# One quarter of each attention pair's products on GpSimd, and a chunk's steps behind the pair's transposes on TensorE

## The reference, cut to what matters

```python
att = softmax(einsum('bhxd,bhyd->bhxy', q, k) * SCALE)
att = softmax(att * mask)            # mask is 0.5 where row % 64 == column % 64, else 1
out = einsum('bhxy,bhyd->bhxd', att, v)
t   = t + (out @ w_out.T + b_out)    # per image, over all 12 heads
```

## Time and profile before

| | |
|---|---|
| runs | 462.84, 463.34, 464.28 us; median 463.34 |
| the profiled execution | 467.23 us, of which 465.4 us are the span from the first to the last instruction |
| busy in the span | PE 425.2 us (91%), DVE 225.7 (48%), ACT 158.6 (34%), POOL 125.3 (27%) |
| first and last second exponential (L691) | 192.21 and 273.38 us: the attention loop is 81 us of the span |
| granted TensorE clock, mean | 0.989 of 2.4 GHz |

### The profile page before, as it was taken

How to read it: one execution, slowest core, us unless ns; L and a number is a source line. 1 busy time by engine, 2 the same in 40 slices (tenths; PEclk the granted TensorE clock), 3 DMA queues, 4 the chain that set the end, 5 groups by cost and what they waited for, 6 DMA issues and landing times.

```text
span 465.4 us, 7581 instructions
## 1 busy us (share of the span) xinstructions
PE 425.2 (91%) x2303; PEld 303.3 (65%) x2304; DVE 225.7 (48%) x611; ACT 158.6 (34%) x399; POOL 125.3 (27%) x136
## 2 busy tenths in 40 slices
PE   0999989999999899988888779998999999999995
PEld 0755356666667888766676547555777777777784
DVE  3536342222222576889889764462533333333333
ACT  1033141222221145988778733211221212221210
POOL 3201044545554000000000000011354444554430
PEclk9999999999999999999999998799999999999999
DMA  8999001111100792000000697600110011100006
GB/s 229 274 311 295 20 24 45 37 38 40 42 23 1 210 355 107 1 0 2 2 1 0 161 241 191 190 10 3 32 34 27 23 29 37 38 28 14 0 0 203
DMA packets 18056, 38.62 MB, mean 83 GB/s; under 512 B 4420, under 2 KB 13892, under 8 KB 17586
## 3 DMA queue, kind: packets, MB, share of 16 engines
q1 hardware_dynamic: 9570, 29.66, 22.6%
q0 software_dynamic: 5280, 6.32, 4.8%
q10 hardware_dynamic: 3184, 2.36, 1.6%
HBM read 35.16 MB, written 7.67 MB: 92 GB/s over the span
## 4 chain that ended last, share of the span: by engine, by line
PE 83%; ACT 6%; DMA 5%; DVE 3%; issue 2%; ACTq 0%; DVEq 0%; SPq 0%; POOLq 0%
PE bank L1250 17%; PE bank L1265 14%; PE bank L1183 12%; PE bank L1244 8%; PE bank L1434 5%; PE bank L1257 4%; PE bank L1388 4%; DMA w_first<-y_rows 3%; PE bank L1450 3%; PE bank L1226 2%; PE bank L1169 2%; PE bank L1482 2%; ACT scratch L691 2%; ACT g_sh L691 2%; ACT xn_t L691 2%
## 5 line engine op out<-in xcount | busy, mean ns | idle before, releaser
L1250 PE MATMUL bank<-w_first,rows_t 96*128 x248 | 85.3, 487 | 0.2 <-issue 0.2
L521 POOL DMA_INDIRECT rows<-xn_rows,slot_tok x56 | 57.3, 1024 | 94.1 <-DVE slot_tok L871 32.5
L529 POOL DMA_INDIRECT y_rows<-y,slot_row x54 | 55.3, 1024 | 98.9 <-DVE y L939 58.3
L1265 PE MATMUL bank<-w_second,hid_t 128*128 x370 | 70.1, 329 | 4.6 <-DVE hid_t L924 2.8
L1265 PEld LDWEIGHTS bank<-w_second,hid_t 128*128 128x128 f32 x370 | 58.7, 190 | 7.1 <-issue 7.0
L1250 PEld LDWEIGHTS bank<-w_first,rows_t 96*128 96x128 f32 x248 | 44.7, 190 | 25.2 <-issue 0.4
L929 DVE TENSOR_TENSOR act_h<-bank,act_g 128x384 f32<-128x384 f32 x31 | 17.3, 558 | 59.1 <-PE bank L1250 59.1
L1244 PE MATMUL bank<-w_first,rows_t 96*128 (+1 forms) x92 | 43.5, 594 | 1.1 <-issue 1.0
L625 ACT ACTIVATE act_g<-bank 128x384 f32<-128x384 f32 x31 | 15.2, 491 | 72.2 <-PE bank L1250 72.2
L941 DVE TENSOR_TENSOR y<-bank,w_second 128x192 f32<-128x192 f32 x23 | 8.2, 358 | 63.7 <-PE bank L1265 63.7
L567 POOL COPY act_h<-o_inv 128x256 f32<-128x256 f32 x12 | 4.8, 402 | 122.3 <-DVE o_inv L1070 122.3
(11 more groups left out here) (181 smaller groups left out, 645.8 us busy)
## 6 DMA issues: line engine op xcount, KB each, us to landing
w_first<-in_gate_up SPq DMA_DIRECT2D x16, 576.0 KB, 9.4
w_second<-in_down SPq DMA_DIRECT2D x1, 4608.0 KB, 19.0
w_first<-in_fc SPq DMA_DIRECT2D x1, 3072.0 KB
w_second<-in_fc SPq DMA_DIRECT2D x1, 3072.0 KB, 28.5
rows<-xn_rows,slot_tok POOLq DMA_INDIRECT x56, 2.6
y_rows<-y,slot_row POOLq DMA_INDIRECT x54, 2.3
w_first<-in_x_t SPq DMA_DIRECT2D x2, 384.0 KB, 4.8
w_first<-in_w SPq DMA_DIRECT2D x1, 768.0 KB, 7.0
```

The source lines that it names most:

```text
L521: pool.indirect_dma_start(rows[b % 2][:], None, xn_rows[L.l], bass.IndirectOffsetOnAxis(slot_tok[:, b:b + 1].bitcast(U32), 0), bounds_chec ...
L529: pool.indirect_dma_start(y_rows[L.l], bass.IndirectOffsetOnAxis(slot_row[:, b:b + 1].bitcast(U32), 0), y[b % 2][:], None, bounds_check=TO ...
L1250: ins = pe.matmul(bank[:, 5 + g, 0:I1], rows_t[0:CH, k, :], w(CH, (k * 2 + g) * I1, I1), start=(k == 0), stop=(k == NCH - 1))
L1265: ins = pe.matmul(bank[:, 1, 0:C], hid_t[:, tile(ic)], w(P, ic * C, C), start=(ic == 0), stop=(ic == L.IC - 1))
```

## The change

- `attention(p)` on DVE does three of the four products. The fourth quarter goes to POOL, as two instructions in place: `fourth(p)` multiplies by the mask (`tensor_tensor`), waits for itself and for DVE's reciprocal, and multiplies by the reciprocal (`tensor_scalar`). POOL's stream alternates `fourth(p)` with the old copy, now `widen(c)`, which stands at odd steps between `fourth(p)` and `fourth(p + 1)`.
- `att_transpose(p)` on PE waits for `p2_ready` and for the three products before its first four transposes, and for the fourth product before its last four.
- PE issues `chunk_stages(p)` behind `att_transpose(p)`, no longer ahead of it. `keep_busy` stays only in the first three steps and behind the loop.
- ACT issues `exp_att(p)` ahead of `out_copy`.
- DVE issues `residual` one step later and `neg_maximum(p + 3)` ahead of `invert_sums` and `out_norm`.

```diff
--- before.py
+++ after.py
@@ -364,6 +364,8 @@
         high_ready, parts_ready = sem("qk_high_part_ready"), sem("qk_parts_ready")
         sc_ps, nmax_ready, e1_ready, att_ready = (
             sem("scores_in_psum"), sem("neg_max_ready"), sem("exp_ready"), sem("att_ready"))
+        exp_inv_ready, masked_ready, fourth_ready = (
+            sem("exp_inverse_ready"), sem("fourth_masked"), sem("fourth_product_ready"))
         att_t_ps, p2_ready, av_ps = sem("att_t_in_psum"), sem("p2_ready"), sem("av_in_psum")
         o_raw_ready, sums_ps, inv_ready, wide_ready, spread_ps = (
             sem("o_raw_ready"), sem("sums_in_psum"), sem("inverse_sums_ready"), sem("inverse_sums_repeated"),
@@ -560,13 +562,29 @@
             nc.gpsimd.tensor_tensor(x_tok[:], x_tok[:], bc(w2_b, 1, [P, NT, C]), ALU.add).then_inc(x_biased, 1)
             pool_blocks(pool, L0)
 
-            for c in range(N_CHUNKS):
+            def fourth(p):
+
+                pool.wait_ge(e1_ready, p + 1)
+                nc.gpsimd.tensor_tensor(e1[p % 3][:, 3, :], e1[p % 3][:, 3, :], mask, ALU.mult
+                                        ).then_inc(masked_ready, 1)
+                pool.wait_ge(masked_ready, p + 1)
+                pool.wait_ge(exp_inv_ready, p + 1)
+                nc.gpsimd.tensor_scalar(e1[p % 3][:, 3, :], e1[p % 3][:, 3, :], exp_inv[:, p % 2, 3:4], None,
+                                        ALU.mult).then_inc(fourth_ready, 1)
+
+            def widen(c):
                 pool.wait_ge(inv_ready, c + 1)
                 if c:
                     pool.wait_ge(spread_ps, c)
                 nc.gpsimd.tensor_copy(o_inv_wide.rearrange("p a g d -> p (a g) d"),
                                       bc(o_inv[:].rearrange("p a g -> p (a g)"), 2, [P, 2 * HPC, HG])
                                       ).then_inc(wide_ready, 1)
+            for p in STEPS:
+                if p < N_PAIRS:
+                    fourth(p)
+                if chunk_at(p, SUMS) is not None:
+                    widen(chunk_at(p, SUMS))
             pool_blocks(pool, L1)
 
 
@@ -718,10 +736,10 @@
                     exp_scores(p + 2)
                 if p == N_PAIRS:
                     act_std(act, 2, 0)
+                if p < N_PAIRS:
+                    exp_att(p)
                 if chunk_at(p, VALUES) is not None:
                     out_copy(chunk_at(p, VALUES))
-                if p < N_PAIRS:
-                    exp_att(p)
 
             act_norm_transposes(act, 2, (0, 1))
             act_std(act, 2, 1)
@@ -1055,11 +1073,14 @@
             def attention(p):
 
                 dve.wait_ge(e1_ready, p + 1)
-                go(v.reciprocal(exp_inv[:, p % 2, :], exp_sum[:, p % 4, :]))
-                for q in range(4):
+                if p >= 2:
+                    dve.wait_ge(fourth_ready, p - 1)
+                v.reciprocal(exp_inv[:, p % 2, :], exp_sum[:, p % 4, :]).then_inc(exp_inv_ready, 1)
+                dve.wait_ge(exp_inv_ready, p + 1)
+                for q in range(3):
                     ins = v.scalar_tensor_tensor(e1[p % 3][:, q, :], e1[p % 3][:, q, :], exp_inv[:, p % 2, q:q + 1],
                                                  mask, ALU.mult, ALU.mult)
-                    if q < 3:
+                    if q < 2:
                         step(ins)
                 ins.then_inc(att_ready, 1)
 
@@ -1092,16 +1113,17 @@
                     neg_maximum(2)
                 if p == N_PAIRS:
                     ln_stats(0)
+                if p and image_at(p - 1) is not None:
+                    residual(image_at(p - 1))
+                if p + 3 < N_PAIRS:
+                    neg_maximum(p + 3)
                 if chunk_at(p, SUMS) is not None:
                     invert_sums(chunk_at(p, SUMS))
                 if p == N_PAIRS + 1:
                     ln_rows(2, 0)
                 if chunk_at(p, SPREAD) is not None:
                     out_norm(chunk_at(p, SPREAD))
-                if p + 3 < N_PAIRS:
-                    neg_maximum(p + 3)
-                if image_at(p) is not None:
-                    residual(image_at(p))
+            residual(IMAGES - 1)
             ln_stats(1)
             ln_rows(2, 1)
             for s in plan[1][1]:
@@ -1427,8 +1449,12 @@
             values(3)
 
             def att_transpose(p):
+                if p:
+                    pe.wait_ge(p2_ready, p)
                 pe.wait_ge(att_ready, p + 1)
                 for m in range(2):
+                    if m == 1:
+                        pe.wait_ge(fourth_ready, p + 1)
                     for kt in range(2):
                         for qt in range(2):
                             ins = pe.transpose(bank[:, 4 + m, (kt * 2 + qt) * P:(kt * 2 + qt + 1) * P],
@@ -1487,9 +1513,8 @@
 
             def chunk_stages(p):
 
-
-                if p:
-                    pe.wait_ge(p2_ready, min(p, N_PAIRS))
+                if p >= N_PAIRS:
+                    pe.wait_ge(p2_ready, N_PAIRS)
                 stages = ((SPREAD, spread_inverses), (VALUES, weigh_values), (SUMS, sums_by_token))
                 for lag, stage_of in stages:
                     if chunk_at(p, lag) is not None:
@@ -1507,10 +1532,12 @@
             for p in range(N_PAIRS):
                 if p + 3 < N_PAIRS:
                     scores(p + 3)
+                if p < 3:
+                    if p:
+                        pe.wait_ge(p2_ready, p)
+                    keep_busy(2)
+                att_transpose(p)
                 chunk_stages(p)
-                if chunk_at(p, VALUES) is None and image_at(p) is None:
-                    keep_busy(2 if p < 3 else 1)
-                att_transpose(p)
 
             chunk_stages(N_PAIRS)
             keep_busy(1)
```

## The result

The changed kernel takes 478.87 us (median of 4 executions, 472.53 to 482.24), the kernel before 463.81: it is slower. The ratio is 1.0235, with a 95% interval of 1.0186 to 1.0284. The falling clock turns out to be part of what the change does, so the median is the fairer number. The profiled execution took 481.08 us, its span 479.3 against 465.4.

The account below looks back on a forecast made before the run. A loop of waits between ACT and PE bounds the kernel; a DVE–PE loop replaces it. Taking turns with POOL adds 4.0 us over twenty pairs, the first steps give -0.7: +3.4 on 463.34, 466.8 us, range 458.5 to 471.

Parts of the forecast that it names:

- The side: Whole kernel: slower than before, chance 0.52, against 0.35 for faster and 0.13 for the same.
- The old loop goes, a new one comes: Attention loop: the ACT–PE loop stops deciding; DVE and PE take turns each step, 6.62 us a chunk against 6.71.
- Taking turns at the reads: DVE products beside POOL's SBUF reads: engines take turns, 0.95 us more a chunk, 466.8 us; chance 0.47.
- POOL's scaling: POOL's multiplication of the fourth quarter by the reciprocal: 0.45 us taken, bounds 0.40 and 0.65.
- The mask: POOL's mask product on the fourth quarter: 0.57 us, 0.65 with an estimated fixed part.
- The sum at full clock: Twenty pairs of the loop taking turns: 75.7 us, +4.0, with -0.7 for the first steps: +3.4.
- The first pairs: First steps of the loop lose a stage ahead of their transposes: about -0.7 us.
- The clock: PE 70 to 80% busy in the loop keeps full clock; a second 1.2 GHz stretch costs 4.8 us, within chance 0.08.
- The signs that it named: Chain through products, sums and spread; chunk near 7.6 us; product gaps or long POOL spans; wrong if POOL's instructions cost far more.

Follow-up runs that it names:

- e3: The change with two keep-busy matmuls ahead of every pair's transposes and all four products back on DVE, POOL only widening: 469.3 us, ratio 1.0101.
- e7: The change's PE and ACT order, four products on DVE, one keep-busy at odd steps, DVE's inversion or normalization one attention later: 456.3 us, ratio 0.9848.
- e11: The change with DVE's inversion or normalization behind the next attention and POOL's widening one step later, no keep-busy matmuls: 457.9 us, ratio 0.9888.
- e5: e1's kernel with POOL's mask and scaling instructions replaced by constant fills of the same quarter: 466.3 us, ratio 1.0064.
- e6: e1's kernel with POOL's scaling also waiting until DVE's three products are done: 475.2 us (one execution).
- e10: The change with the old order's keep-busy matmuls, one at odd steps and none at even ones: 476.1 us, ratio 1.0267.
- e1: The change with two keep-busy matmuls ahead of every pair's transposes: 471.2 us, ratio 1.0141.
- e2: The kernel before, without its keep-busy matmuls from step 3 on: 465.9 us, ratio 0.9963.
- e4: The kernel before, in its old order with its keep-busy matmuls, with the fourth quarter on POOL: 462.9 us, ratio 0.9962.
- e8: e7's kernel with the fourth quarter on POOL as in the change and the widening one step later: 455.6 us, ratio 0.9824.

## Why the prediction was wrong, point by point

The side was right. The sum that it was made of comes near the kernel at full clock, in part by luck, since two mis-sized terms offset each other. The time was not right: 466.8 forecast, up to 471.0 in the range, 478.9 measured, and what failed is the clock, the fifth point below.

- **The old loop goes, a new one comes: right.** The change's own chain is the drawn one in both kinds of step. With four products the step behind the sums was put at 3.67, and e3 has 3.73 with the widening's 0.18 in it; e3's chunk of 7.54 against 7.4 proves less, because keep-busy matmuls set its other step. e7 and e11 show it from the other side: with DVE's wait taken out they are 13.0 us below e3 (some of it keep-busy matmuls that e3 has on its chain and e7 has not) and 21.6 below the change. The call that the reordering makes a wait that gives its gain back was this prediction's best step.
- **Taking turns at the reads: the mechanism right, the rule too strong.** The step behind the widening was put at 3.27 + 0.95 = 4.22 and measured 4.02. The two engines do not take turns in full: instructions that take 1.28 and 0.92 alone run side by side in 1.50 and 1.14, so each loses 0.22, where full exclusion would have made 2.2 of the two. Of what the Trainium skill says on its page "SBUF — State Buffer", "Who interferes with whom", two things agree with the runs: two SBUF inputs on DVE collide with a POOL instruction that reads and not with one that only writes (e5), and a reduction is safe beside POOL (1.21 for the maximum over PSUM beside the mask, 1.17 to 1.22). The Trainium skill calls the shared ports there an exclusive lock; the 1.50 and 1.14 don't agree with that.
- **POOL's scaling: mis-sized.** 0.45 was taken, with 0.65 as the upper bound; it is 0.92 alone (e6). The copy was the wrong neighbour, and so was the price of two tensor inputs. The mask was put at 0.65 and is 0.73. The longer scaling offsets the point above in one step and makes the other 3.51 for 3.35: 1.6 us too little over ten steps there, 1.4 too much over the seven of 4.22. That they cancel is luck.
- **The sum at full clock.** With the steps as the change and e10 show them, pairs 4 to 23 are 10 x 3.51 + 7 x 4.02 + 3 x 4.09 = 75.5 against 71.65: +3.9. The first pairs give 0.1 and not 0.7 (exp_att of pair 0 to pair 4: 12.95, before 13.08). That is +3.7, or 467.5, 0.7 us from the forecast. No run shows the whole kernel at this clock with no keep-busy matmuls on the chain, so it stays an estimate; e1 less the 5.2 of its own matmuls gives 466.0, and the line through the change's ten executions 466.1.
- **The clock: the step that failed.** "In the new loop PE is busy 5.8 - 0.54 = 5.3 of 6.6 to 7.6 us, 70 to 80%, which those rows show at full clock" took a mean over 10 us of the old trace as a licence. The changed kernel's clock has a mean of 0.81 in the loop, with stretches at the lower of its two levels (1.2 GHz, 0.50 in 225 to 230). A projection that begins at that level takes 2.77 us (229.88, mean 0.76) for 2.06, and a chunk 9.08 (242.20 to 251.28, mean 0.69) for 7.53. The remaining 11 of the 15 us are this: 478.9 less 467.5, or 13 by the two lower estimates. e1 shows the cause: the same loop with matmuls in PE's waits keeps 1.00 and is 7.6 us shorter, though those matmuls cost it 5.2. The prediction had the clock only as one stretch behind the loop worth 4.8 us, with a share of a chance of 0.08, and booked the removed keep-busy matmuls as 0.54 of gain a step. e2 shows that their removal costs the old order about as much as it gains.
- **The signs that it named** pointed at the forecast: the chain runs through the products, a chunk takes 7.53 for 7.6, and POOL's scaling takes 1.14. One sign of being wrong came true as well: both of POOL's instructions cost far more than a third of a microsecond. None of the signs was of the clock.

The failed step depends on the right ones. In the old loop PE waited 0.45 us at a time and 1.1 at most; the turn-taking and POOL's share made that 1.9. The clock then lengthens the very steps on which DVE waits, and e11 shows that without the turn-taking most of it goes, even with no keep-busy matmuls (0.97 from 190 to 290). What it takes in PE's work to hold the clock stays open: e2's clock falls with waits no longer than those of the kernel before.

## What to carry to other kernels

When a stage is moved behind another on one engine, follow who consumes it: if the consumer stands ahead of the producer's own input in a third engine's order, two engines that overlapped now take turns. Moving the consumer one step down, too, was worth 21.6 us here (e11, with what it did for the clock), while the work taken off the engine was worth 0.4% in the old order (e4, its interval ends at 0.7%) and nothing clear of noise in the repaired one (e8 against e7). Before giving POOL elementwise work, look what DVE runs at that moment: an instruction with two SBUF tensors lengthens both, a reduction over PSUM doesn't. And matmuls that keep TensorE busy are not free to remove while the waits that they fill remain: here that cost more than it gained (e1 against the change).

## What was not expected of the hardware

- A 128 by 256 float32 `tensor_scalar` with a per-partition factor took POOL 0.92 us alone, against 0.73 for a `tensor_tensor` with the mask (beside the maximum over PSUM), 0.40 for a copy and 0.31 for a fill.
- A shorter POOL instruction can cost DVE more: the two-tensor form took 0.85 beside three products and lengthened them by 0.35, the per-partition form 1.14 and 0.22.
- TensorE's granted clock fell from 1.00 to 0.50 in a loop where PE had been busy 3.5 and 3.1 of 5 us and never waited longer than 1.9, and in the old order without keep-busy matmuls, where it was busier (4.1 of the 5 us ahead of the first fall, to 0.73) and never waited longer than 1.1. It fell at different moments in the change's two profiles (0.83 and 0.50 in 210 to 220), and by different amounts in its ten executions (means of 0.933 to 0.982), which spread the same kernel's times over 16 us.
